# A four-stage transformer kernel: the preparation of the second attention moved beside the last chunk's experts, its last norm into the first head's tiles

## The reference

```python
x = x + _layernorm(_L0_attn_ref(_layernorm(x), W_qkv, W_out))              # 16 heads of 64
x = x + _layernorm(_L0_ffn_ref(_layernorm(x), ...))                        # shared + 8 experts, top 2
x = x + _layernorm(_L1_attn_ref(_layernorm(x), Wq, Wk, Wv, Wo, lambda_*, rms_scale))
x = x + _layernorm(_L1_ffn_ref(_layernorm(x), ...))                        # ternary weights
# in _L1_attn_ref, 8 heads of 2 x 128:
lam = (exp(sum(lambda_q1 * lambda_k1)) - exp(sum(lambda_q2 * lambda_k2)) + LAMBDA_INIT)
attn = softmax(A1) - lam * softmax(A2)          # A1, A2: scaled scores of the two maps
O = attn @ V;  O = O / rms(O) * rms_scale * (1 - LAMBDA_INIT);  out = O @ Wo
```

## Time and profile before

| what | value |
|---|---|
| median of three runs | 2038.34 us (2037.19 to 2041.45) |
| the profiled execution | 2038.1 us |
| its span in the trace | 2036.3 us |
| TensorE busy (matmuls) | 1941.5 us, 95% |
| VectorE / ScalarE / GpSimd busy | 75% / 68% / 55% |
| granted TensorE clock, mean | 0.984 |

### The profile page before, as it was taken

One profiled execution on the slowest core, in us unless ns is written; L12 is line 12 of the kernel. 1 busy time (PEld: TensorE's weight loads), 2 busy tenths in 40 slices (PEclk: granted clock), 3 DMA queues, 4 the chain that ended last, 5 costly groups with the idle time before them and its releaser, 6 DMA issues.

```text
span 2036.3 us, 37994 instructions
## 1 busy us (share of the span) xinstructions
PE 1941.5 (95%) x12066; PEld 1669.8 (82%) x12066; DVE 1518.0 (75%) x2604; ACT 1378.1 (68%) x2641; POOL 1122.8 (55%) x1361
## 2 busy tenths in 40 slices
PE   4999999999999999899998999999999999999688
PEld 3888888888888888689997788888888888888566
DVE  5988898889898989643223777777777777777575
ACT  3878787878787878544443677777777777776355
POOL 3655555555555555320001677777777777778521
PEclk9999999999999999999999999999999999999699
DMA  4212111111111111100000000000000000100000
GB/s 113 48 44 48 43 46 43 46 43 46 43 46 43 46 43 45 47 14 1 1 1 1 9 3 12 1 10 0 10 0 10 0 10 0 65 1 1 1 5 17
DMA packets 37766, 51.22 MB, mean 25 GB/s; under 512 B 8489, under 2 KB 17714, under 8 KB 37426
## 3 DMA queue, kind: packets, MB, share of 16 engines
q1 hardware_dynamic: 37682, 50.15, 9.7%
HBM read 15.52 MB, written 1.05 MB: 8 GB/s over the span
## 4 chain that ended last, share of the span: by engine, by line
PE 84%; DVE 6%; issue 4%; ACT 3%; POOL 2%; DMA 1%; SPq 0%; ACTq 0%; DVEq 0%; POOLq 0%
PE ps_t L546 7%; PE ps_o L556 7%; PE ps_t L1018 6%; PE ps_o L557 5%; PE ps_s L578 5%; PE ps_s L579 5%; PE ps_s L1354 5%; PE ps_s L1355 5%; PE ps_s L1356 5%; PE ps_t L1408 3%; PE ps_o L1422 3%; PE ps_o L1424 3%; PE ps_o L1423 3%; PE ps_s L999 2%; PE ps_s L1000 1%
## 5 line engine op out<-in xcount | busy, mean ns | idle before, releaser
L1558 DVE TENSOR_REDUCE a_negmax<-ps_s 128x1 f32<-128x1024 f32 x256 | 312.4, 1220 | 67.3 <-PE ps_s L1356 64.7
L720 DVE TENSOR_REDUCE a_negmax<-ps_s 128x1 f32<-128x1024 f32 x256 | 313.5, 1224 | 52.5 <-PE ps_s L579 37.7
L1486 ACT ACTIVATE a_p<-ps_s,a_negmax 128x1024 f32<-128x1024 f32 x256 | 286.5, 1119 | 95.2 <-DVE a_negmax L1558 94.1
L655 ACT ACTIVATE a_pth<-ps_t 128x512 fp32r<-128x512 f32 x512 | 278.7, 600 | 91.4 <-PE ps_t L546 91.2
L706 DVE TENSOR_TENSOR a_ptl<-ps_t,a_pth 128x512 fp32r<-128x512 f32 x512 | 327.6, 681 | 6.5 <-ACT a_pth L655 5.5
L783 POOL TENSOR_SCALAR a_p<-a_p,a_rsum 128x1024 f32<-128x1024 f32 x256 | 289.4, 1130 | 52.8 <-POOL a_rsum L779 52.8
L1659 POOL TENSOR_TENSOR a_p<-a_p 128x1024 f32<-128x1024 f32 x128 | 307.7, 2404 | 10.7
L779 POOL TENSOR_TENSOR a_rsum<-a_sum,minus_one 128x1 f32<-128x1 f32 x256 | 141.4, 552 | 306.7 <-ACT a_p L685 305.5
L685 ACT ACTIVATE a_p<-ps_s,a_negmax 128x1024 f32<-128x1024 f32 x256 | 288.6, 1127 | 15.2 <-DVE a_negmax L720 15.2
L546 PEld LDWEIGHTS ps_t<-ident_r,a_pr 128*128 128x128 f32 x2048 | 200.4, 140 | 32.0 <-POOL a_p L783 4.0
L556 PE MATMUL ps_o<-a_pth,a_v 128*128 128x512 f32 x512 | 220.4, 431 | 3.6 <-ACT a_o L664 2.2
(11 more groups left out here) (228 smaller groups left out, 4537.7 us busy)
## 6 DMA issues: line engine op xcount, KB each, us to landing
a_q<-a_kh SPq DMA_DIRECT2D x64, 128.0 KB, 2.2
a_q<-a_kl SPq DMA_DIRECT2D x64, 128.0 KB, 2.3
a_kh<-a_kh SPq DMA_DIRECT2D x64, 128.0 KB, 2.2
a_kl<-a_kl SPq DMA_DIRECT2D x64, 128.0 KB, 2.3
a_w_raw<-in_l_w SPq DMA_DIRECT2D x8, 384.0 KB, 3.0
f_raw<-in_ffn_w SPq DMA_DIRECT2D x2, 1408.0 KB, 7.8
f_w_raw<-in_ffn_w SPq DMA_DIRECT2D x9, 256.0 KB, 5.7
f_w<-in_ffn_w SPq DMA_DIRECT2D x9, 256.0 KB, 4.3
```

The source lines that it names most:

```text
L720: dve.tensor_reduce(a0_negmax[:, s % 4:s % 4 + 1], ps_s[:, s % 2, :, :], AX.XY, ALU.max, negate=True)\
L1558: dve.tensor_reduce(a1_negmax[:, s % 2, m:m + 1], ps_s[:, m, :, :], AX.XY, ALU.max, negate=True)\
```

## The change

The prologue of a1 moves into the last chunk of f0: after each position `pos` of chunk 3, TensorE, ScalarE and VectorE do a piece of it. The turns of chunks 0, 1 and 2 come at positions 2, 3 and 8, the weights at 4, their product and the lambda sum at 5, the query pieces at 6 and 7, in the banks ps_m and ps_o. GpSimd splits the keys of chunks 0 to 2 right behind the norm of each. The heads begin behind the last expert without a prologue. The norm of chunk 3 then runs in slots 0 and 1 of head 0: VectorE keeps the statistics, while GpSimd applies the norm and adds it to X (both were VectorE's). TensorE turns chunk 3 in slot 3 of head 0, and GpSimd splits its keys and clears Y there; the last two query pieces of batch 1 move from slots 2 and 3 to slots 4 and 6 of head 0. The four query pieces are numbered by half first. The other heads keep their slots. ScalarE's loop over the chunks ends one round earlier, and the last round is written out.

```diff
+                    if c == NC - 1:
+                        a1_pe_prepare(pe, pos)
...
+                    if isinstance(c, int) and c == NC - 1:
+                        a1_act_prepare(act, pos)
                 if start:
                     f0_act_probs(act, 1)
             f0_act_w1_hi(act, 1)
             chunk(0, True)
-            with act.Fori(1, NC) as c:
+            with act.Fori(1, NC - 1) as c:
                 chunk(c, False)
+            chunk(NC - 1, False)
...
-            c, n = NC - 1, NORM_F0 + 2 * (NC - 1)
-            add_experts(c)
-            dve.wait_ge(S["a1_lam_loaded"], 16)
-            lam = a1_lam[:, :, :].rearrange("p (m w) h -> p m w h", w=2)
-            dve.tensor_tensor(a1_lprod[:, :, :], lam[:, :, 0, :], lam[:, :, 1, :], ALU.mult)\
-                .then_inc(S["a1_lprod_ready"], 1)
-            norm_stats(dve, n, 0, y_of(c))
-            turn_dve(dve, TURN_F0, 0, ps_t[:, 0, :])
-            step(norm_apply(dve, n, 0, y_of(c), lambda i: tile(xhat, i)))
-            a1_dve_am(dve, 0, ps_m)
-            xc = X[:, c * TPC:(c + 1) * TPC, :]
-            step(dve.tensor_tensor(xc, xc, xhat[:, :, :], ALU.add))
-            x_tile = lambda i: tile(X, c * TPC + i)
-            norm_stats(dve, n + 1, 1, x_tile)
-            turn_dve(dve, TURN_F0 + 1, 1, ps_t[:, 1, :])
-            norm_apply(dve, n + 1, 1, x_tile, y_of(c)).then_inc(S["x1_ready"], 1)
-            turn_dve(dve, TURN_F0 + 2, 2, ps_t[:, 0, :])
-            dve.wait_ge(S["a1_lexped"], 1)
-            step(dve.tensor_tensor(a1_neglam[:, :], a1_lexp[:, 1, :], a1_lexp[:, 0, :], ALU.subtract))
-            step(dve.tensor_scalar(a1_neglam[:, :], a1_neglam[:, :], -LAMBDA_INIT, None, ALU.add))
+            c = NC - 1
+            a1_dve_prepare(dve, 0)
+            add_bias(c)
+            for pos in range(1, NE):
+                add_expert(c, pos)
+                a1_dve_prepare(dve, pos)
+            dve.wait_ge(S["f0_added"], c * NE + NE)
+            dve.sem_inc(S["waited"], 1)
...
-            with pool.Fori(0, NC) as c:
-                pool_steps.enter(c, 2)
+            for c in range(NC - 1):
                 norm_rstd(pool, c * 2 + NORM_F0, 0)
                 norm_rstd(pool, c * 2 + (NORM_F0 + 1), 1)
-                pool_steps.leave(NC)
+                a1_keys(pool, c)
...
-        Q_PIECES = [(m, half) for m in range(2) for half in range(2)]
+        Q_PIECES = [(m, half) for half in range(2) for m in range(2)]
+        Q_SECOND = ((0, 1, 2, 3), (0, 1, 4, 6))
+        X_SLOT = 3
         NQ = len(Q_PIECES)
-        def a1_q_piece(s, last):
-            if s < NQ:
-                return 1, *Q_PIECES[s]
+        def a1_q_piece(s, first, last):
+            if s in Q_SECOND[first]:
+                return 1, *Q_PIECES[Q_SECOND[first].index(s)]
...
+        def a1_pe_turn(pe, c, bank):
+            pe.wait_ge(S["x1_ready"], c + 1)
+            if c:
+                pe.wait_ge(S["x_lo"], TURN_F0 + c)
+            turn_pe(pe, TURN_F0 + c, c, lambda i: Y[:, c * TPC + i, :], bank)
+        A1_TURNS = (2, 3, NE - 1)
+        A1_WT = 4
+        A1_QUERIES = {6: (0, 1), 7: (2, 3)}
+        def a1_pe_prepare(pe, pos):
+            if pos in A1_TURNS:
+                if pos == NE - 1:
+                    pe.wait_ge(S["a1_q_lo"], NQ)
+                a1_pe_turn(pe, A1_TURNS.index(pos), ps_m)
+            elif pos == A1_WT:
+                pe.wait_ge(S["x_lo"], TURN_F0 + 2)
+                pe.wait_ge(S["f0_added"], (NC - 1) * NE + 1)
+                a1_pe_wt(pe, 0, 0, ps_m)
+                a1_pe_wt(pe, 0, 1, ps_o)
+            elif pos == A1_WT + 1:
+                a1_pe_am(pe, 0, ps_m)
+                pe.wait_ge(S["a1_lprod_ready"], 1)
+                pe.matmul(ps_o[:, 0:2 * H1], ones[:, :], a1_lprod[:, :, :], start=True, stop=True)\
+                    .then_inc(S["a1_lsum_in"], 1)
+            elif pos in A1_QUERIES:
+                if 0 in A1_QUERIES[pos]:
+                    pe.wait_ge(S["a1_am_lo"], 1)
+                    pe.wait_ge(S["a1_lexped"], 1)
+                else:
+                    pe.wait_ge(S["a1_q_lo"], 2)
+                for i in A1_QUERIES[pos]:
+                    a1_pe_q(pe, (0, *Q_PIECES[i]), (ps_m, ps_o)[i % 2][:, :])
+        def a1_act_prepare(act, pos):
+            if pos in A1_TURNS:
+                c = A1_TURNS.index(pos)
+                turn_act(act, TURN_F0 + c, c, 1.0, ps_m[:, :])
+            elif pos == A1_WT:
+                a1_act_wt(act, 0, 0, ps_m)
+                a1_act_wt(act, 0, 1, ps_o)
+            elif pos == A1_WT + 1:
+                a1_act_am(act, 0, ps_m)
+                act.wait_ge(S["a1_lsum_in"], 1)
+                act.activation(a1_lexp[:, :, :], ps_o[:, 0:2 * H1].rearrange("p (m h) -> p m h", m=2), ACT.Exp)\
+                    .then_inc(S["a1_lexped"], 1)
+            elif pos in A1_QUERIES:
+                for i in A1_QUERIES[pos]:
+                    a1_act_q(act, i + 1, (0, *Q_PIECES[i]), (ps_m, ps_o)[i % 2][:, :])
+        def a1_dve_prepare(dve, pos):
+            def step(ins):
+                ins.then_inc(S["dve_step"], 1)
+                dve.wait_ge(S["dve_step"], dve_steps.next())
+            if pos + 1 in A1_TURNS:
+                c = A1_TURNS.index(pos + 1)
+                turn_dve(dve, TURN_F0 + c, c, ps_m[:, :])
+            if pos == 0:
+                dve.wait_ge(S["a1_lam_loaded"], 16)
+                lam = a1_lam[:, :, :].rearrange("p (m w) h -> p m w h", w=2)
+                dve.tensor_tensor(a1_lprod[:, :, :], lam[:, :, 0, :], lam[:, :, 1, :], ALU.mult)\
+                    .then_inc(S["a1_lprod_ready"], 1)
+            elif pos == A1_WT:
+                a1_dve_am(dve, 0, ps_m)
+                dve.wait_ge(S["a1_lexped"], 1)
+                step(dve.tensor_tensor(a1_neglam[:, :], a1_lexp[:, 1, :], a1_lexp[:, 0, :], ALU.subtract))
+                step(dve.tensor_scalar(a1_neglam[:, :], a1_neglam[:, :], -LAMBDA_INIT, None, ALU.add))
+            elif pos + 1 in A1_QUERIES:
+                for i in A1_QUERIES[pos + 1]:
+                    a1_dve_q(dve, i + 1, (0, *Q_PIECES[i]), (ps_m, ps_o)[i % 2][:, :])
+        def a1_keys(pool, c):
+            pool.wait_ge(S["x1_ready"], c + 1)
+            b, tiles = c * TPC // KT, slice(c * TPC % KT, c * TPC % KT + TPC)
+            y = Y[:, c * TPC:(c + 1) * TPC, :]
+            pool.tensor_scalar(a1_xh[b][:, tiles, :], y, 1.0, 0.0, ALU.mult, ALU.add).then_inc(S["a1_xh_ready"], 1)
+            pool.wait_ge(S["a1_xh_ready"], c + 1)
+            pool.tensor_tensor(a1_xl[b][:, tiles, :], y, a1_xh[b][:, tiles, :], ALU.subtract)\
+                .then_inc(S["a1_xk_ready"], 1)
+        X1_CHUNK, X1_NORM = NC - 1, NORM_F0 + 2 * (NC - 1)
+        def x1_stats(dve, i):
+            if i:
+                dve.wait_ge(S["x1_summed"], 1)
+            norm_stats(dve, X1_NORM + i, i, lambda k: tile((Y, X)[i], X1_CHUNK * TPC + k))
+        def x1_apply(pool, i):
+            norm_rstd(pool, X1_NORM + i, i)
+            pool.wait_ge(S["norm_rstd"], X1_NORM + i + 1)
+            pool.sem_inc(S["waited"], 1)
+            for k in range(TPC):
+                t = X1_CHUNK * TPC + k
+                dst, src = (tile(xhat, k), tile(Y, t)) if i == 0 else (tile(Y, t), tile(X, t))
+                ins = pool.tensor_scalar(dst, src, mv[:, i, k, 0:1], rstd[:, i, k:k + 1], ALU.subtract, ALU.mult)
+            ins.then_inc(S["x1_applied" if i == 0 else "x1_ready"], 1)
+            if i == 0:
+                pool.wait_ge(S["x1_applied"], 1)
+                xc = X[:, X1_CHUNK * TPC:(X1_CHUNK + 1) * TPC, :]
+                pool.tensor_tensor(xc, xc, xhat[:, :, :], ALU.add).then_inc(S["x1_summed"], 1)
         def a1_pe(pe):
-            a1_pe_wt(pe, 0, 0, ps_m)
-            a1_pe_wt(pe, 0, 1, ps_o)
-            a1_pe_am(pe, 0, ps_m)
-            pe.wait_ge(S["f0_added"], NC * NE)
-            pe.wait_ge(S["a1_lprod_ready"], 1)
-            pe.matmul(ps_o[:, 0:2 * H1], ones[:, :], a1_lprod[:, :, :], start=True, stop=True)\
-                .then_inc(S["a1_lsum_in"], 1)
-            def turn(c):
-                pe.wait_ge(S["x1_ready"], c + 1)
-                turn_pe(pe, TURN_F0 + c, c, lambda i: Y[:, c * TPC + i, :])
-            for c in range(NC - 1):
-                turn(c)
-            pe.wait_ge(S["a1_am_lo"], 1)
-            pe.wait_ge(S["x_lo"], TURN_F0 + 2)
-            for i, (m, half) in enumerate(Q_PIECES):
-                a1_pe_q(pe, (0, m, half), first_bank(i))
-            turn(NC - 1)
-            pe.wait_ge(S["x_lo"], TURN_F0 + NC)
-            pe.wait_ge(S["a1_lexped"], 1)
-            pe.wait_ge(S["a1_xk_ready"], NC)
...
+                if first and s == X_SLOT:
+                    pe.wait_ge(S["a1_q_lo"], a1_q_done(h, s - 1, first))
+                    pe.wait_ge(S["a1_pt_lo"], 2 * (X_SLOT - LAG_TURN))
+                    a1_pe_turn(pe, NC - 1, spare)
+                    return
...
+                if first and s == 0:
+                    pe.wait_ge(S["f0_added"], NC * NE)
```

(33 more changed lines are left out.)

61 lines of the change are left out of this document (26 added, 35 removed).

## The result

The changed kernel has a median of 2031.6 us (2029.7 to 2032.4, six runs); 2028.3 us was forecast. The ratio to the kernel before, measured beside it, is 0.9959 with the interval [0.9945, 0.9973]. In five more runs it was 2031.3 us, ratio 0.9965 [0.9951, 0.9979]. By these ratios it is faster by 8.4 and 7.1 us, where 9.8 were forecast. The profiled execution took 2029.7 us; its span in the trace is 2027.9 us, against 2036.3 before.

The account below looks back on a forecast made before the run. TensorE, busy 95% of the span, was taken as the bound, so its idle hole before the heads counts. 11.7 - 0.3 - 1.6 = 9.8 us off 2038.1 gives 2028.3 us, range 2026.0 to 2032.2.

Parts of the forecast that it names:

- The hole: Between the last expert and the first scores: 18.1 us with little TensorE work, which the change was to close.
- rival D: Last expert chunk: in-order queues make each preparation position a 2.0 us round trip, 14 us, ending at 2042.3 us; chance 0.03.
- Part 1: Preparation moved into the last expert chunk: costs TensorE 6.4 us (lower end 5.6), first scores 11.7 us earlier.
- Part 2: Last norm beside the first slots of head 0: 0.3 us later at slot 4 than before, bounds 0 to 0.8.
- Four applications at 0.36 us each: GpSimd's norm applications in head 0's first slots, ending 5.8 us after the first scores.
- in time for the second statistics at 8.9: GpSimd's sum in head 0 ends at 7.2 us after the first scores, before VectorE's second statistics at 8.9.
- from here both go at the same pace: After tile 1's second exponential, 13.4 us after the first scores, slots run as before, 5.2 us each.
- Rival A: Head 0, slots 1, 2, 4: VectorE's factor waits for whole GpSimd instructions, 3.8 us in all, giving 2032.1 us; chance 0.08.
- the 2.81 us of VectorE's applications: Kernel before, last norm: four applications beside GpSimd's key splits, 1.11 us with GpSimd idle; explained by the shared-port lock.
- Rival B: Head 0, slots 1 to 3: TensorE's clock falls, costing 1.8 us, to 2.5 with a second slot; 2030.8 us; chance 0.08.
- Part 3: Query pieces moved into full slots 4 and 6 of head 0: 0.8 us lost each, 1.6 together, bounds 1.2 and 1.9.

Follow-up runs that it names:

- one_pointer: Changed kernel with the second pointer scalar, rstd, replaced by a constant 1.0 in GpSimd's norm applications of chunk 3; one run, 2027.5 us.
- forms: Changed kernel with the four GpSimd applications of each group in different arithmetic (two products, or a difference then a product, with pointers or constants); one run, 2027.8 us.
- forms_again: Changed kernel with each group's four GpSimd applications in other orders of product, sum and difference, all with two pointer scalars; one run, 2027.7 us.
- each half alone: Changed kernel with only the preparation beside the experts, ratio 1.0002 to the kernel before; or only the norm in head 0's slots, preparation behind the experts, 1.0024.

## Why the prediction was right or wrong

**Direction and kind: right.** The hole closes and TensorE pays for the preparation with its own length. No position became a round trip (rival D): TensorE is busy 10.00 of 10 us in each stretch from 1040 to 1110 of the changed kernel.

**Part 1: size off, in the change's favour.** The preparation cost 5.4 us, not 6.4, just below the lower end of 5.6. The row of a group of transposes is longer than the time for which it holds up the next matmul: the turn at 1104.07 has 0.60 us, and the down-projection starts 0.43 us behind it. The three turns took 1.2 us of TensorE together instead of 1.8, the six weight tiles 0.6 instead of 0.9, their product and the lambda sum 0.6 instead of 0.9; only the query pieces took a little more, 3.0 instead of 2.8. With the hole of 18.2 us, taken from the start of the last down-projection's last matmul, the first scores came 12.8 us earlier, not 11.7.

**Part 2: the step that failed.** "Four applications at 0.36 us each" is the term that was mis-sized: the row is of the same engine, operation name and size, but of two products, and the change has a difference and a product, 0.79 us. The prediction gave this term no bounds, though the rows of before show no GpSimd application of this arithmetic. With it fell "in time for the second statistics at 8.9" (they began at 9.9, behind 0.94 us of waiting) and "from here both go at the same pace". Slot 6 came at 38.0 and 36.6 us, where 33.4 were forecast (32.3 + 0.3 + 0.8 for the piece in slot 4). Only 0.8 us of this excess had arisen when the second exponential of tile 1 ended (14.2 for 13.4); the larger part came behind it, where the same pace was assumed: from there to slot 6 it took 23.9 and 22.4 us, and 19.1 before. With four applications at 1.74 us, near the 1.44 forecast, slot 6 comes at 34.3, and with the factor's wait gone too at 33.7, with 20.4 us behind that exponential (19.1 + 1.1 forecast). This shows the cause, and leaves 0.3 us open.

**Rival A: the right mechanism, half the price.** The factor waited 1.66, 0.76 and 0.34 us more than its 0.22, at 1128, 1135 and 1142, so 2.8 us in the trace. It is worth 1.4 to 2.8 us in slot 6, against 3.8 forecast; with the clock held it is worth 0.8, and in the kernel with short applications 0.6. The two causes feed each other: with GpSimd late, its sums lie where the factors fall. The time forecast for A (2032.1) is near the median, but for a sum of two causes. The Trainium skill's rule ("SBUF — State Buffer", section "SBUF: two separate sides") has it that a VectorE instruction with two SBUF inputs takes part in the lock; the factor's 1.88 us agrees, and so does its 0.27 us with one tensor input. By the same section it contends with any GpSimd instruction that reads SBUF. The trace agrees beside one large instruction with a single input tensor, and the kernel before already showed it, near the end of its last head:

```profile
1874.55 0.99 POOL L1745 TENSOR_SCALAR f_w<-f_raw 128x939 fp32r<-128x939 f32 x1
1874.80 0.75 DVE L1571 SCALAR_TENSOR_TENSOR a_c<-a_rsum,a_sum,a_neglam 128x1 f32<-128x1 f32 x1
```

The factor ends where that instruction ends, and so it does in all twelve executions with the old factor (0.73 to 0.77 us). These rows answer what the prediction calls open, whether the wait holds for the factor. Beside small instructions the trace differs from the rule, and the measurement decides: within the power L316 the factor took its usual 0.22 us, and beside the applications too, in seven executions. Five of these seven factors began in the last 0.11 us of an application, so they say little; two began well within one (`one_pointer`, `forms`), and waited for nothing. In an eighth execution (`forms_again`) such a factor took 0.29. Which instructions of GpSimd hold the factor, and which don't, stays open.

The prediction also takes the 2.81 us of VectorE's applications for an instance of two SBUF inputs. Each of them reads one tensor and two pointer scalars, and the one-input factor, which reads the same, never waited. So the number of inputs doesn't explain the 2.81 us, and no run here shows what does.

**Rival B: the event, its price open.** The clock fell as described, and holding it gained nothing in slot 6 in three pairs of kernels (36.6 with the clock held against 38.0 and 36.6 in the changed kernel's two executions, then 35.8 against 35.2 and 36.1 against 36.1). The second exponential of tile 2 ended at 19.8 us where it fell in slot 2 and at 19.2 where it didn't, in the changed kernel's two executions too. So 0.6 us is the price at that point, against 1.8 forecast; the idle matmuls may have hidden what of it reaches slot 6.

**Part 3: right in kind, a little low.** Slot 6 took 5.44 us before and 6.40 with the piece, so 1.0 us more instead of 0.8, and 5.43 again in the kernel that has the pieces in slots 0 to 3. From the start of its scores to that of the next, slot 4 took 5.0 us before and 6.1 in the kernels where little else disturbs it (the one-input factor with the short applications, or with one application), so about 1.1. The whole length from slot 6 on, +1.2 and +0.7 us, can't show this: it came out +1.1 in the kernel without a piece in slot 6.

Balance, forecast and the two executions: first scores -11.7, -12.8 and -12.8; up to slot 6 +1.1, +5.7 and +4.3; behind it +0.8, +1.2 and +0.7. Sum -9.8, -5.9 and -7.8. The forecast charged too much for the preparation and too little for the slots, and the two errors cancelled in part: that the median missed by only 3.3 us is partly luck.

## What to carry to other kernels

Two stretches that hide each other can give their gain only together: each half alone, as written here, was worth nothing or less (1.0002, 1.0024). Before work goes to an engine where it has not yet run, find a row of the same arithmetic, not only of the same operation and size, or carry both ends into the range. If a rival asks whether an instruction can be held up, look at its longest row in the trace of before, not at its median. And write GpSimd's subtraction of a scalar from a tensor as the addition of its negative, where the small instruction that negates it (0.25 us here) is repaid.

## What the runs showed of the hardware

- GpSimd's TENSOR_SCALAR on 128x128 fp32 with two pointer scalars: with a difference, at either place, 0.80 us; with sums and products 0.45. A pointer scalar in place of a constant costs 0.08. A TENSOR_TENSOR difference of 128x512 (L1392, 1.28) costs as much as a sum (L1416, 1.28), so it is not the subtraction as such.
- A VectorE instruction of one element a partition can hold its engine for 1.88 us when it reads two tensors from SBUF beside GpSimd's two-tensor sum, and for 0.75 us beside a one-tensor instruction of 128x939. Beside the power L316 (two tensors of four elements, 1.04 us) it took its usual 0.22, and within an application of 128x128 too, so not every GpSimd instruction holds it. With one tensor and two pointer scalars it never waited in 128 cases. That isn't a rule for every one-tensor instruction: the applications L307 of the kernel before have one tensor too and took 2.81 us beside key splits.
- One kernel's clock falls came at different slots in different executions (1122 to 1126 and 1132 to 1136, or 1116 to 1122). Idle matmuls kept the clock at 1.00 and didn't bring slot 6 forward.
